# A two-layer graph network kernel: the second layer's supertiles of five tiles become supertiles of four, with base nodes of their own

## The reference, cut to what matters

```python
h = jnp.maximum(_layernorm(x), 0.0)
x = x + segment_sum(h[src] * edge_weight[:, None], dst)            # layer 0
h = jnp.maximum(_layernorm(x), 0.0)                                # layer 1
hid = relu(edge_attr_32 @ W1 + b1)                                 # 32 -> 64, per edge
w = (hid @ W2 + b2).reshape(e, 4, 8, 8)                            # 256 weights per edge
w_000, w_011, w_101, w_110 = w[:, 0], w[:, 1], w[:, 2], w[:, 3]
s_e, v_e = s[src], v[src]                                          # 8 scalars, 8 vectors of 3
m0 = 0.25 * (einsum(s_e * sh0, w_000) + C110 * einsum(v_e, sh1, w_110))
m1 = 0.25 * (einsum(s_e, sh1, w_011) + einsum(v_e * sh0, w_101))
x = x + segment_sum([m0, m1], dst) + self_interaction(h)
```

## Time and profile before

| | |
|---|---|
| median of three runs | 6678.94 us |
| the profiled execution, its own time | 6675.92 us |
| its span, first to last instruction | 6674.1 us |
| granted PE clock, mean | 0.992 of 2.4 GHz |
| PE busy | 6489.0 us (97%) |
| DVE busy | 5619.0 us (84%) |
| POOL busy | 4878.7 us (73%) |
| ACT busy | 2966.1 us (44%) |
| layer 0 / between / layer 1 | about 0 to 2,920 / to 2,974 / to 6,640 us |

### The profile page before, as it was taken

One profiled execution on the slowest core, in us unless ns is written; L12 is line 12 of the kernel. 1 busy time (PEld: TensorE's weight loads), 2 busy tenths in 40 slices (PEclk: granted clock), 3 DMA queues, 4 the chain that ended last, 5 costly groups with the idle time before them and its releaser, 6 DMA issues.

```text
span 6674.1 us, 156533 instructions
## 1 busy us (share of the span) xinstructions
PE 6489.0 (97%) x40552; PEld 4418.8 (66%) x40552; DVE 5619.0 (84%) x14128; ACT 2966.1 (44%) x12673; POOL 4878.7 (73%) x5214
## 2 busy tenths in 40 slices
PE   6999999999999999979999999999999999999998
PEld 5888888888888888855555555555555555555554
DVE  7887777777777777769999999999999999999997
ACT  2222222222222222245555555555555555555555
POOL 5777777777777777767777777777777777777775
PEclk9999999999999999979999999999999999999998
DMA  4111111111111111111111111111111111111111
GB/s 106 34 32 33 32 32 32 32 32 33 32 32 32 32 32 32 33 38 36 34 33 34 35 34 33 34 35 34 33 34 35 34 33 34 35 34 33 34 34 32
DMA packets 331940, 235.18 MB, mean 35 GB/s; under 512 B 109833, under 2 KB 328281, under 8 KB 331405
## 3 DMA queue, kind: packets, MB, share of 16 engines
q0 software_dynamic: 163424, 84.00, 9.0%
q1 hardware_dynamic: 167500, 147.69, 8.2%
q10 hardware_dynamic: 990, 3.21, 0.2%
HBM read 229.28 MB, written 5.23 MB: 35 GB/s over the span
## 4 chain that ended last, share of the span: by engine, by line
PE 62%; POOL 26%; issue 10%; DVE 1%; POOLq 1%; DMA 1%; SPq 0%; ACT 0%; DVEq 0%; ACTq 0%
POOL z L457 26%; PE hp_ps L821 15%; PE sc_ps L795 12%; PE w_ps L780 10%; PE w_ps L770 7%; PE w_ps L701 6%; PE w_ps L789 5%; PE w_ps L776 3%; PE w_ps L786 2%; PE w_ps L800 1%; PE w_ps L711 0%; POOLq L454 0%; PE hp_ps L711 0%; DMA x_sb<-in_x 0%; DMA z<-h_table,idx 0%
## 5 line engine op out<-in xcount | busy, mean ns | idle before, releaser
L457 POOL DMA_INDIRECT z<-h_table,idx x5107 | 4834.7, 947 | 1711.4 <-issue 1576.3
L701 PE MATMUL w_ps<-parts,pick 128*128 128x448 f32 x11662 | 2537.2, 371 | 59.2 <-DVE pick L1014 57.4
L701 PEld LDWEIGHTS w_ps<-parts,pick 128*128 128x128 f32 x11662 | 2143.9, 188 | 245.1 <-issue 57.4
L559 ACT ACTIVATE z<-z,squares 128x32 f32<-128x32 f32 x3125 | 736.5, 309 | 2064.4 <-DMA z<-h_table,idx 1945.9
L821 PE MATMUL hp_ps<-parts,pick 128*128 128x448 f32 x4340 | 1044.7, 380 | 0.0
L610 ACT ACTIVATE hid<-w_ps,b_sb 128x320 f32<-128x320 f32 x625 | 329.5, 527 | 1525.3 <-PE w_ps L770 1525.2
L821 PEld LDWEIGHTS hp_ps<-parts,pick 128*128 128x128 f32 x4340 | 766.7, 188 | 251.9 <-issue 205.9
L1014 DVE TENSOR_TENSOR pick<-sc_ps,feat 128x896 fp32r<-128x896 f32 x833 | 889.1, 1088 | 48.8 <-issue 43.6
L795 PE MATMUL sc_ps<-prod,onehot 128*32 128x344 f32 x6250 | 842.0, 463 | 4.3 <-DVE reduced_sb L1144 4.3
L1174 DVE TENSOR_TENSOR prod<-w_ps,coef 128x192 f32<-128x192 f32 x1250 | 808.7, 647 | 0.3 <-ACT coef L617 0.3
L654 ACT ACTIVATE near<-iota_sb,rel_sb 128x32 f32<-128x32 f32 x3125 | 722.4, 309 | 0.0
(11 more groups left out here) (92 smaller groups left out, 5078.8 us busy)
## 6 DMA issues: line engine op xcount, KB each, us to landing
z<-h_table,idx POOLq DMA_INDIRECT x5107, 2.4
feat<-key_table SPq DMA_DIRECT2D x311, 192.0 KB
ft_sh_sb<-in_ft_sh SPq DMA_DIRECT2D x313, 180.0 KB
feat<-key_table SPq DMA_DIRECT2D x210, 64.0 KB
h_table<-big SPq DMA_DIRECT2D x10, 280.0 KB
rel_sb<-in_dst_t SPq DMA_DIRECT2D x1, 1562.5 KB, 12.0
idx_all<-in_src_t SPq DMA_DIRECT2D x1, 1532.5 KB, 8.3
squares<-in_ew_t SPq DMA_DIRECT2D x1, 1532.5 KB, 11.7
```

The source lines that it names most:

```text
L457: pool.indirect_dma_start(z[:, r, u, :], None, rows, bass.IndirectOffsetOnAxis(ap=idx[:, r, u:u + 1], axis=0)).then_inc(z_in[r], 16)
L559: last = nc.scalar.activation(z[:, r, u, :], z[:, r, u, :], ACT.Copy, scale=ew_all[:, bass.ds(n * G + u, 1)])
L701: mm = pe.matmul(fold_ps[:, pick_banks[k], 0:NC * D], pick[:, k, blk, :], parts[:, t, :, blk, :], start=(blk == 0 and t == 0), stop=(blk = ...
```

## The change

Layer 1 runs in S1 = 782 supertiles of G1 = 4 tiles; 3 tiles of padding with destinations that match no node are added. Layer 0 keeps its 625 of five. Layer 1 gets base nodes, spans, keys and relative destinations of its own: least and greatest destination per tile are computed at the start (the same reads of `dst_flat`), go out to DRAM and come back in groups of four, and are reduced at the end of layer 0; after layer 0, SP loads `dst_t` into `rel_sb` a second time, with the new base table, and the DVE subtracts (`window_slots1`) after the second normalisation and ahead of `add_si`. `last_weights` and the fifth tile's own DVE operations go. `wts_ready` is raised by `weights`; `fold_sums` gets a semaphore of its own, `fold1_ready`, and waits for `acc1_done`. Every even supertile still has one tile gathered on PE (of four). The keys of layer 1 stand together in the key table, so that a load of three takes consecutive rows. `dst_t` is loaded behind the first keys. The number of keys rises from 833 to 1,224.

```diff
-HALF = SUP // 2
+G1 = 4
+SUP1 = G1 * P
+HALF1 = SUP1 // 2
+GT1 = G1 - 1
...
-        prod_flat = sb("prod", [P, 3 * G * TILE])
+        prod_flat = sb("prod", [P, 3 * G1 * TILE])
...
-            full = S // ring - written_out
+            full = count // ring - written_out
...
         def load0(b, r, s):
             if s == 0:
                 load_tables()
-                sp.dma_start(rel_sb[:].bitcast(I32), dst_t).then_inc(dstt_in, 16)
                 sp.wait_ge(key_out, 16 * len(in_rows(KP)))
             if r % BATCH == 0:
                 load_keys(b, r, s)
+            if s == 0:
+                sp.dma_start(rel_sb[:].bitcast(I32), dst_t).then_inc(dstt_in, 16)
...
+            sp.wait_ge(acc0_done, S)
+            sp.dma_start(rel_sb[:].bitcast(I32), dst_t).then_inc(dst1_in, 16)
+            sp.wait_ge(tab1_out, 32 * len(in_rows(SPP1)))
+            sp.dma_start(span1_row, span1_dram.rearrange("(a s) -> a s", a=1)).then_inc(span1_in, 16)
+            sp.dma_start(base_bc[:], base1_dram.rearrange("(a s) -> a s", a=1).to_broadcast([P, S1])).then_inc(base1_in, 16)
+            sp.dma_start(base_row[:], base1_dram.rearrange("(a s) -> a s", a=1)).then_inc(base1_in, 16)
...
             def load_keys1(first, count):
-                sp.dma_start(key1[:, 0:count, :], key_dram[bass.ds(first, count, 2)].rearrange("s a e -> a s e")
+                sp.dma_start(key1[:, 0:count, :], key_dram[bass.ds(first, count)].rearrange("s a e -> a s e")
                              .to_broadcast([P, count, P])).then_inc(keys1_in, 16)
...
-            def last_weights(q):
-                rows = slice(64, 67)
-                pe.matmul(w_ps[:, 0, 2, 0:WN], ones_sb[rows, :], b2_rows[rows, 0:WN], start=True, stop=False)
-                for k in range(2):
-                    half = slice(k * HID, (k + 1) * HID)
-                    mm = pe.matmul(w_ps[half, 0, 2, 0:WN], hid[half, q, 2 * P:HALF], w2_sb[half, :], start=False, stop=True)
-                return mm
             def window_sums(r, v):
-                for u in range(G):
-                    k = u % 4
-                    mm = pe.matmul(sums_ps[k * WIN:(k + 1) * WIN, :], onehot[:, r, u, :], prod[:, v, u],
-                                   start=(u < 4), stop=(u > 0))
+                for u in range(G1):
+                    mm = pe.matmul(sums_ps[u * WIN:(u + 1) * WIN, :], onehot[:, r, u, :], prod[:, v, u], start=True, stop=True)
...
-                    weights(q)
+                    weights(q).then_inc(wts_ready, 1)
...
-                if s is None or 1 <= s <= S:
-                    pe.wait_ge(last_wts_used, n)
-                elif s > S:
-                    pe.wait_ge(acc1_done, n - 4)
                 if s is None or s >= 4:
                     pe.wait_ge(sum1_reduced, n - 3)
-                    total = fold_sums(q)
-                if s is None or s < S:
-                    last_weights(q).then_inc(wts_ready, 1)
+                    if s is None or s >= 5:
+                        pe.wait_ge(acc1_done, n - 4)
+                    fold_sums(q).then_inc(fold1_ready, 1)
...
+            def window_slots1():
+                dve.wait_ge(span1_in, 16)
+                nc.vector.tensor_reduce(span_max[:, 1:2], span1_row, AX, ALU.max).then_inc(span_ready, 1)
+                dve.wait_ge(dst1_in, 16)
+                dve.wait_ge(base1_in, 32)
+                nc.vector.tensor_tensor(rel_sb[:].rearrange("p (s g) -> p s g", g=G1), ...
...
             normalise(1, CH - 1)
+            window_slots1()
...
-                scalar_products(last_wts_ps, last_tile)
+                wts = wts_ps[q]
+                nc.vector.tensor_tensor(
+                    p011[:], wts[:, :, 2 * MUL:3 * MUL].rearrange("p (g o) i -> p g o i", o=MUL),
+                    scalars[:, q].unsqueeze(2).to_broadcast([P, G1, MUL, MUL]), ALU.mult).then_inc(prod_step, 1)
                 dve.wait_ge(coef_ready, n + 1)
-                vector_rows(last_wts_ps, last_tile)
+                shape = [P, G1, MUL, 3, MUL]
+                nc.vector.tensor_tensor(
+                    vector_out,
+                    wts[:, :, 3 * MUL:4 * MUL].rearrange("p (g i) o -> p g i o", i=MUL).unsqueeze(3).to_broadcast(shape),
+                    cf[:, :, 2:5].rearrange("p (g i) m -> p g i m", i=MUL).unsqueeze(4).to_broadcast(shape), ALU.mult)
                 take()
                 step(2)
-                scalar_rows(last_wts_ps, last_tile).then_inc(last_wts_used, 1)
-                scalar_products(wts_ps[q], first_tiles).then_inc(prod_step, 1)
-                vector_rows(wts_ps[q], first_tiles)
-                scalar_rows(wts_ps[q], first_tiles).then_inc(wts_used, 1)
+                shape = [P, G1, MUL, 2, MUL]
+                nc.vector.tensor_tensor(
+                    scalar_out,
+                    wts[:, :, 0:2 * MUL].rearrange("p (g i) (b o) -> p g i b o", i=MUL, b=2),
+                    cf[:, :, 0:2].rearrange("p (g i) b -> p g i b", i=MUL).unsqueeze(4).to_broadcast(shape), ALU.mult
+                    ).then_inc(wts_used, 1)
                 select()
...
                 def take():
                     if s is None or s >= 4:
+                        dve.wait_ge(fold1_ready, n - 3)
                         take_sums(n - 4, None if s is None else s - 4, first_column(n - 4), acc1_done, total1_ps)
...
-    src_pe = np.concatenate([a["src"].reshape(S, G, P)[:, G - 1], a["src"].reshape(S, G, P)[PERIOD - 1::PERIOD, G - 2]])
+    src_pe = np.concatenate([a["src"].reshape(S, G, P)[:, G - 1], a["src"].reshape(S, G, P)[PERIOD - 1::PERIOD, G - 2],
+                             src1.reshape(S1, G1, P)[::2, G1 - 1]])
```

More of the change, by code:

```diff
@@ L253, in gnn_two_layers, with supertiles @@
             sem(n) for n in ("prod_step", "msg1_ready", "sum1_ready", "sum1_reduced", "acc1_done"))
-        def supertiles(eng, ring, body, lag=0, written_out=0):
-            full = S // ring - written_out
+        def supertiles(eng, ring, body, lag=0, written_out=0, count=S):
+            full = count // ring - written_out
             for s in range(ring):
@@ L262, in supertiles @@
                     body(b, r, None)
-            for s in range(full * ring, S + lag):
+            for s in range(full * ring, count + lag):
                 body(s // ring, s % ring, s)
@@ L388, in _ @@
+                    sp.wait_ge(tiles_out, 32 * (len(in_rows(SPP)) + (T1 > T)))
+                    for to, dram in ((tiles1_least, tile_least_dram), (tiles1_most, tile_most_dram)):
+                        for lot in in_rows(SPP1):
+                            sp.dma_start(to[lot], dram.rearrange("(p k) -> p k", p=SPP1)[lot]).then_inc(tiles1_in, 16)
             supertiles(sp, R0, load0)
             def wide_loads(layer, loads):
-                with if_wide(sp):
-                    with sp.Fori(0, S) as n:
+                g, count = per_tile[layer], per_count[layer]
@@ L399, in _ @@
-            wide_loads(0, [])
+                    sp.wait_ge(wide_free[layer], count + 1)
+            sp.wait_ge(tables1_ready, 2)
+            for lot in in_rows(SPP1):
+                sp.dma_start(base1_dram.rearrange("(p k) -> p k", p=SPP1)[lot], least1_i[lot]).then_inc(tab1_out, 16)
+                sp.dma_start(span1_dram.rearrange("(p k) -> p k", p=SPP1)[lot], span1_i[lot]).then_inc(tab1_out, 16)
+            wide_loads(0, [])
+            sp.wait_ge(acc0_done, S)
+            sp.dma_start(rel_sb[:].bitcast(I32), dst_t).then_inc(dst1_in, 16)
@@ L468, in wide_gathers @@
             def wide_gathers(layer, rows, loads):
-                with if_wide(pool):
-                    with pool.Fori(0, S) as n:
+                with if_wide(pool, layer):
+                    with pool.Fori(0, per_count[layer]) as n:
                         pool.wait_ge(wide_in[layer], (n + 1) * 16 * loads)
                         pool.nop(nofuse=True)
-                        for u in range(G):
+                        for u in range(per_tile[layer]):
                             pool.indirect_dma_start(
@@ L479, in pool_stages @@
             def pool_stages(layer):
-                pool.wait_ge((acc0_done, acc1_done)[layer], S)
-                with if_wide(pool):
-                    pool.wait_ge(wide_free[layer], S + 1)
+                pool.wait_ge((acc0_done, acc1_done)[layer], per_count[layer])
+                with if_wide(pool, layer):
+                    pool.wait_ge(wide_free[layer], per_count[layer] + 1)
                 def stage_share(n, k, first, g):
@@ L495, in tiles1 @@
             def tiles1(r, s):
-                return GT if on_pe(r) and (s is None or s >= R1) else G
-            supertiles(pool, R1, gathers(R1, h1_dram, idx1_ready, z1_in, msg1_ready, tiles1), written_out=1)
+                return GT1 if on_pe(r) and (s is None or s >= R1) else G1
+            supertiles(pool, R1, gathers(R1, h1_dram, idx1_ready, z1_in, msg1_ready, tiles1), written_out=1, count=S1)
             wide_gathers(1, h1_dram, 3)
@@ L647, in edge_rows @@
```

(14 more changed lines are left out.)

296 lines of the change are left out of this document (160 added, 136 removed).

## The result

The changed kernel takes 6754.39 us, median of four runs (6751.89 to 6756.17), against 6678.78 us before (6677.61 to 6679.98). The ratio is 1.0113, 95% interval 1.0095 to 1.013: slower by 76 us. The forecast was 6748 us, slower by 69.

The account below looks back on a forecast made before the run. PE bounds it now; after the change the DVE, 27.0 us per block plus 1.6 key wait, makes layer 1 3727 us, 66 more. With +3 outside the loop, 6679 + 66 + 3 = 6748 us; range 6630 to 6800.

Parts of the forecast that it names:

- PE: Layer 1 matmuls: 1.48 us less per supertile, so PE needs 26.3 us per block of six.
- the rival in which PE stays the bound: Fifth tile's rounds in layer 1 already hidden, 0.58 us per supertile stays, time 6896 us; chance 0.05.
- DVE: Layer 1 operations summed by starts: 27.0 us per block of six, making the DVE the bound by a little.
- the forecast's estimate with that cost as an occupancy: 120 cycles per PSUM-reading DVE instruction would add 1.9 us per pair, layer 1 above 4200 us; the forecast rejected it.
- The key wait: At each layer 1 block boundary the DVE idles 1.6 us for SP's key load; bounds 0.7 and 1.97.
- The rival in which the keys come in time: Keys at layer 1 block boundaries land 2.4 us after issue, idle 0.7, time 6631 us; chance 0.2.
- the forecast's estimate of 2.45 us: Landing of the 192 KB key load by the skill's fit; would make the kernel faster, about 6637 us.
- PE's clock: Rival: PE's clock falls in layer 1's new idle, about 2 us in 28.6; chance 0.02.
- PE and DVE catching on each other: Rival in layer 1: 0.5 us more per block beside the keys, 65 us more, 6813 us; chance 0.08.
- The forecast's own sign for it: DVE waits for L795, PE's window sums in layer 1, of more than 0.2 us would show coupling.
- A second sign: PE idle for 7 to 9% of layer 1, with waits for L1004 or L1143/L1144, if the forecast is right.
- Outside the loop: `window_slots1`, second `dst_t` load and start-up reductions around the layers: +3 us together, bounds 0 and 8.

Follow-up runs that it names:

- fifth run: Changed kernel with keys asked for early and the group's one-hot moved from the DVE to two ACT operations: 6450.39 us, ratio 0.9656.
- first run: Changed kernel with the key load put ahead of the wait for the features' buffer: 6503.31 us, ratio 0.9732 to the kernel before.
- fourth run: Kernel before, with its key load put ahead of the wait for the features' buffer: 6683.23 us, ratio 1.0001.
- second run: Changed kernel with keys issued ahead of the features, after the same wait for the DVE's last product: 6659.36 us, ratio 0.9966.
- third run: Changed kernel with eight extra matmuls per block, read by nothing, in PE's idle: 6729.79 us, ratio 1.007.

## Why the prediction was right, point by point

- **PE.** Forecast 26.3 us per block; 26.30 where PE binds, in the fifth run. In the rows, the way from the start of the window sums to L823 fell from 2.86 to 1.38 us, by the 1.48 that the forecast took off. That the fifth tile costs two whole rounds of its column group was read rightly: the rival in which PE stays the bound falls.
- **POOL.** Seven gathers per pair as forecast: 2201 / 7 = 314.4 pairs in 3000 us, 9.54 us each. It never bound; by the forecast's sum it stands at 26.2, right behind PE.
- **DVE.** Forecast 27.0 us per block, measured 26.68. The method (starts, not lengths) held. The Trainium skill, "VectorE: DVE Perf Modes", section on the TRN2 errata, gives an instruction that reads PSUM a fixed cost beside its elements; the forecast's estimate with that cost as an occupancy came to above 4200 us, which the trace does not bear out. The term was 0.3 us too large. In the first run's timeline L1221 gives way to L1228 after 0.45 us, where I took 0.485 for L1160 and L1163 with four tiles, and L1040 to L1240 after 0.09 and not 0.11:

```profile
5004.19 0.25 DVE L1221 TENSOR_TENSOR vsh<-z,ft_sh_sb 128x96 f32<-128x96 f32 x1
...
5004.64 0.42 DVE L1228 TENSOR_TENSOR p<-w_ps,scalars 128x256 f32<-128x256 f32 x1
...
5005.84 0.17 DVE L1040 TENSOR_TENSOR acc<-acc,w_ps 32x32 f32 x1
5005.93 0.67 DVE L1240 TENSOR_TENSOR prod<-w_ps,coef 128x512 f32<-128x512 f32 x1
```

  Six times 0.05 to 0.055 is 0.30 to 0.33: the whole of it. Two thirds of the first error is a slip of the sum: L1160 and L1163 both lose 24 elements, and the sum took them off once. Worth 42 us on 130 blocks.
- **The key wait.** Forecast 1.6 us per block, on the path in full; measured 1.77. The pick starts 3.42 us after the keys' issue over all boundaries, where 3.3 was taken, and the DVE gets from the block's last product to the pick in 2.84 us (first run), not 2.875. Worth 22 us. The rival in which the keys come in time falls. How long the keys take alone on the queue is shown by the runs that ask for them early; the landing is 3.1 us, in the kernel before (fourth run, every second row of the key table) and in the changed one (fifth run, consecutive rows):

```profile
feat<-key_table SPq DMA_DIRECT2D x86, 192.0 KB, 3.1
```

```profile
feat<-key_table SPq DMA_DIRECT2D x113, 192.0 KB, 3.1
```

  At a boundary the two loads are 288 packets in the changed kernel and 544 before, as the forecast expected, but that brought no earlier landing. The Trainium skill, "DMA: Bandwidth & Descriptors", section "Anatomy of one DMA — SWDGE (gpsimd) path", gives its fit for DMAs that GpSimd issues, and SyncE issues this one; the forecast's estimate of 2.45 us by it does not agree with the 3.1 us here.
- **PE's clock.** Here the forecast was wrong in kind. It took the clock as nothing and, as a rival with a chance of 0.02, as a general fall. It was in between: short dips in about a quarter of the blocks, 25 us. The forecast leaned on layer 0, whose idle is 73 us in 2600 at a clock of 1.00. In the changed layer 1 PE is idle for 150 us in 3000, with one piece of mostly 0.8 to 1.1 us per block. In the second run, without a dip, it is 110 us, and the longest piece of a block is mostly 0.6 us or less, though above 0.7 in 12 of 107. Whether the length of the pieces or their sum decides is not shown.
- **PE and DVE catching on each other.** At full clock: not seen. The forecast's own sign for it, waits of the DVE for the window sums of more than 0.2 us, did appear, 29 times and up to 0.7 us; it is the dips, since in the third run, with the clock at 1.00, none is left. The slack covers PE at full clock and not at half. A second sign was off too: PE's idle was to be 7 to 9% and is 5.0%. As an estimate, PE's work in 29 times 3.4 us at half clock counts some 50 us, 1.6%, more as busy; the rest is open.
- **Outside the loop.** Forecast +3 (of it 1 to 4.3 for `window_slots1`), measured about +4 as the difference 76 - 72, 3.7 at the first landmark and 4.1 at the first pick.

Together -42 + 22 + 25 + 1 = +6 on the forecast of 69: 75, against 76 measured. The mechanism was forecast; that the time came within 7 us is in part luck, because the DVE's term was too large by about as much as the key wait and the clock together were too small.

## What to carry to other kernels

Cutting work from the engine that is full pays only down to the next chain, and that chain need not be an engine. List, for each wait that is hidden now, how long it would be if the engine in front of it came as early as the change lets it: here a load asked for inside the supertile that uses it, and hidden before by PE's window sums, cost 231 us. The change loses 1.1% with it, gains 2.7% without it, and 3.4% with one more operation moved off the DVE. A load's request belongs behind the wait for its own buffer, not behind an unrelated one that happens to be ahead of it on the same queue.

## What the runs showed of the hardware that was not expected

In the changed kernel PE was idle for 5% of layer 1, with one piece of mostly 0.8 to 1.1 us in a block of 28.6, and in about every fourth block its granted clock fell to 1.2 GHz for 3.4 us. With eight matmuls that nobody reads put into that idle (0.98 us per block) the clock stayed at 2.4 GHz, and the kernel was 25 us faster. And of two loads issued one behind the other on SyncE's queue the second was hardly later for it (3.42 against 3.38 us from issue to use); what it paid is the 0.5 us by which SyncE issued it later.
